# Layer-0 attention scores: one 128-column matmul per head over 64 contraction rows, in place of one 256-column matmul per pair of heads over 128 rows

## The chip, the cores and the metric

The kernel runs on one core of a Trainium2 chip. The metric is the device time of one execution in microseconds (us).

## What is computed

A two-layer Perceiver block, batch 1: 128 queries of width 256 attend to a context of 12544 positions of width 192. Each of the two layers has cross attention, a small self attention and a feed-forward part. The change touches only the cross attention of layer 0 (16 heads of 16 channels, no mask):

```python
x = x + _L0_xattn_ref(_layernorm(x, axis=-1), ctx_768, Wq, bq, Wk, bk, Wv, bv, Wo, bo)

def _L0_xattn_ref(query, key_value, Wq, bq, Wk, bk, Wv, bv, Wo, bo):
    q = (query @ Wq + bq)        # split into 16 heads of 16
    k = (key_value @ Wk + bk)
    v = (key_value @ Wv + bv)
    attn = jnp.einsum('bhqd,bhkd->bhqk', q, k) * scale
    attn = jnp.clip(attn, -CLAMP, CLAMP)
    attn = jax.nn.softmax(attn, axis=-1)
    x = jnp.einsum('bhqk,bhkd->bqhd', attn, v)
    return x @ Wo + bo
```

## The kernel before

The program is written by hand, one instruction stream for each engine, with named semaphores (S["..."]) between them.

**Layer 0 in chunks.** The context is worked through in 14 chunks (NCH) of 896 positions (CH), each chunk in 7 tiles (TPC) of 128 positions. While the scores of chunk c are computed, chunk c+1 is prepared: keys are projected (`project0`, L1319) and values (`values0`, L1326), and an upper estimate of every head's maximum is taken by 32 small matmuls (`unit_scores`, L1336, each over the 32 rows of one pair of heads, 448 columns) whose results VectorE reduces (`unit_max`, L899). The maxima of the chunk go through a matmul (`minus_max_row`, L1345) and a ScalarE copy (`max_row`, L625) into rows of the score operand `qs`, so that the matmul of the scores subtracts them.

**Scores.** Operands are split in a rounded high part and a rest, both kept in the type fp32r. In `ks` and `qs` the products high*high, high*low and low*high are stacked along the contraction: rows 0 to 31, 32 to 63 and 64 to 95 hold the 2 x 16 channels of a pair of heads in three versions, rows 96 to 127 hold ones against the negated maxima. So `scores0` (L1413 to L1421) needs a single matmul per pair of heads: 128 rows, 128 positions (the weights, from `ks`), and 256 columns (the queries of both heads; the queries of the other head are zero in a head's columns). A tile has 8 such matmuls in two halves (z), each half filling two PSUM banks; ScalarE takes the exponential of the two banks in one instruction (`exponentials`, L666).

**Weighing.** `weigh0` (L1430) multiplies the exponentials with the values in plain fp32, which the chip executes as two instructions per matmul: 16 matmuls of 17 weight columns a tile, four of them side by side in the column groups of the array.

**Order.** The table LIST (L76 to L78) sets the order of TensorE's work: S is the scores of the next tile, W the weighing of this one, m one maximum matmul, K, V, F, R, L the other preparing steps. Three PSUM banks (5 to 7) are used in turn by all of K, V, m, F, R and L. In the five middle steps the order is

```python
LIST += [["S", "m", "m", "m", "W", "m", "m"]] * 5
```

in the first step S stands between two K (after K1, before K2), and in the last step it stands behind L and before the next chunk's K0. In that last place the two halves of S each wait (`e0_top`) for ScalarE's copies of the maxima.

**Moving keys to their rows.** A DMA can put data in any partition, so SyncE's queue fills `ks`: `stack_keys` (L313 to L325) issues 12 DMAs a chunk of 32 partitions each (L323), 8 when the high parts of the keys are ready (`e0_khi`) and 4 when the low parts are (`e0_klo`). Behind them on the queue are the loads of a later chunk (`load_sum0`) and the way of the maxima to all partitions (`spread_max`), which only a rarely used clipping path reads. `qs` is filled once by 12 DMAs (L309). GpSimd sets the rows of ones in both halves of `ks` by two memsets (L473, L490).

Of the kernel before, what the change touches and what calls it, by code (L numbers as in the profile page):

```python
# [150 lines left out]
def perceiver(nc, a, out):  # L151
    with ExitStack() as ctx:
# [15 lines left out]
        qs = sb("qs", [P, HQ], F32R)  # L168
# [111 lines left out]
        def _(sp):  # L280
# [26 lines left out]
            for slot, part in ((0, qp[:, :, :, :]), (1, qp_lo), (2, qp[:, :, :, :])):  # L307
                for g in range(4):
                    sp.dma_start(qs_v[32 * slot:32 * slot + 32, :, g, :].bitcast(F32),  # L309
                                 part[32 * g:32 * g + 32].rearrange("p t e q -> p t (e q)").bitcast(F32)  # L310
                                 ).then_inc(S["qs_rows"], 16)

            def stack_keys(c, b):  # L313
# [3 lines left out]
                sp.wait_ge(S["e0_score"], HALVES * (c + 1))  # L317
                for slot, part in ((0, 0), (1, 0), (2, 1)):
                    if slot == 2:
                        carry_wait()  # L320
                        sp.wait_ge(S["e0_klo"], 4 * c + 4)
                    for g in range(4):
                        sp.dma_start(ks_v[32 * slot:32 * slot + 32, b, g::4, :].bitcast(F32),  # L323
                                     khl[32 * g:32 * g + 32, part, :, :].bitcast(F32)
                                     ).then_inc(S[f"e0_keys{b}"], 16)  # L325

            def spread_max(c):
# [4 lines left out]
                sp.dma_start(rows_d, qs[96:97, :].bitcast(F32)).then_inc(S["e0_row_out"], 16)  # L332
# [93 lines left out]
        def _(pool):  # L426
# [50 lines left out]
            pool.wait_ge(S["qs_rows"], 192)  # L477
# [12 lines left out]
            nc.gpsimd.memset(ks[96:P, GROUPS * CH:].bitcast(F32), 1.0).then_inc(S["ks_ones"], 1)  # L490
            pool.wait_ge(S["ks_ones"], 2)
# [85 lines left out]
        def _(act):  # L577
# [81 lines left out]
            def exponentials(c, b, t):  # L659

                for u in (2 * t, 2 * t + 1):
                    g = HALVES * c + u
                    act.wait_ge(S["e0_ok"], g + 1)
                    act.wait_ge(S["e0_score"], g + 29)
# [6 lines left out]
            def chunk0(c, b, i2, nxt=True, split=True, sums=False):  # L671

                for t in range(TPC):
                    for kind, i, n in STEPS[t]:
# [9 lines left out]
                        elif kind == "K":  # L684
                            if i == 0:
                                act.wait_ge(S[f"e0_keys{b}"], 192 * (i2 + 1))
# [6 lines left out]
                        elif kind == "R":  # L693
                            if i % 2 == 0:
                                act.wait_ge(S["e0_score"], HALVES * (c + 1) + 27 + i // 2)
# [1038 lines left out]
```

## Time and profile before

| | |
|---|---|
| median of 3 runs | 980.12 us (979.84 to 983.88) |
| the profiled execution: its own time | 981.7 us |
| its span, first to last instruction | 979.9 us |
| TensorE busy (matmul) | 832.2 us, 85% |
| VectorE / ScalarE / GpSimd busy | 646.0 / 426.7 / 217.2 us |
| mean granted TensorE clock | 0.915 of full speed |

Layer 0's chunks fill the span from about 60 to 531 us; the rest is layer 1 and the short stages between. A duration in the profile is that of one instruction from its start to its end; matmuls overlap, so that their rate is read from when a row of n like instructions starts and how long it lasts, and not from the mean duration.

### The profile page before, as it was taken

What the parts mean: (1) busy time and instruction counts of PE and PEld (TensorE: products, weight loads), DVE (VectorE), ACT (ScalarE), POOL (GpSimd) and SP (SyncE); (2) the same over time, 40 slices, a digit from 0 to 9 for tenths busy, and PEclk for the clock granted to TensorE, in tenths of its full rate; (3) what the DMA queues carried; (4) which work ended last, traced back from release to release, by engine and by line L of the source; (5) the groups of instructions that cost most, each with busy time, mean ns of one, the idle gap of its engine ahead of it and who ended that gap; (6) DMA issues with size and microseconds to landing.
All of it is one profiled execution on the core that took longest, in us unless ns stands there. A gap on an engine that the chain in (4) does not pass through costs nothing. (4 is left out here: it accounts for less than half of the span.)

```text
span 979.9 us, 21240 instructions
## 1 busy us (share of the span) xinstructions
PE 832.2 (85%) x7299; PEld 640.1 (65%) x7299; DVE 646.0 (66%) x1116; ACT 426.7 (44%) x575; POOL 217.2 (22%) x234
## 2 busy tenths in 40 slices
PE   3889999999999999999996166995999999996605
PEld 2567777777777777777775055653788888885304
DVE  5767766856766676676664123895577877785782
ACT  2246676576666667666666022100233323331011
POOL 4162102202211220220104902140132223220000
PEclk9779999999999999999999568997899999998755
DMA  5845654573565557386333003200000000000000
GB/s 169 204 135 126 157 148 127 117 181 104 135 156 138 133 115 177 104 229 156 92 88 113 39 0 124 76 13 0 13 12 18 18 13 17 18 13 0 1 0 6
DMA packets 44152, 85.35 MB, mean 87 GB/s; under 512 B 11648, under 2 KB 26945, under 8 KB 42177
## 3 DMA queue, kind: packets, MB, share of 16 engines
q1 hardware_dynamic: 44110, 84.87, 33.6%
q8 instruction: 18, 0.29, 0.1%
q14 instruction: 24, 0.19, 0.1%
HBM read 45.27 MB, written 0.25 MB: 46 GB/s over the span
## 5 line engine op out<-in xcount | busy, mean ns | idle before, releaser
L899 DVE TENSOR_REDUCE cu<-ps 128x1 f32<-128x448 f32 x448 | 250.4, 618 | 53.2 <-PE ps L1336 51.3
L666 ACT ACTIVATE pr<-ps 128x1024 f32<-128x1024 f32 x196 | 190.1, 1023 | 64.9 <-PE ps L1418 64.1
L432 POOL TENSOR_TENSOR pause<-pause 128x1 f32<-128x1 f32 x41 | 13.0, 317 | 584.7 <-DVE mr L911 376.9
L1418 PE MATMUL ps<-qs,ks 128*128 128x256 f32 x784 | 122.9, 296 | 5.8 <-ACT qs L625 3.1
L1336 PE MATMUL ps<-khl,qp 32*128 32x448 f32 x448 | 123.4, 480 | 3.0 <-DVE khl L889 0.9
L1418 PEld LDWEIGHTS ps<-qs,ks 128*128 128x128 f32 x784 | 102.0, 190 | 24.4 <-issue 20.0
L1430 PE MATMUL ps<-pr,v 128*17 128x128 f32 x3136 | 104.7, 274 | 0.6 <-DVE ps L976 0.5
L1585 PE MATMUL ps<-ks,ct 128*128 128x512 f32 x352 | 99.5, 405 | 2.7 <-ACT ks L769 2.3
L1430 PEld LDWEIGHTS ps<-pr,v 128*17 128x17 f32 x3136 | 77.2, 97 | 22.5 <-issue 19.2
L1336 PEld LDWEIGHTS ps<-khl,qp 32*128 32x128 f32 x448 | 57.5, 186 | 48.8 <-DVE cu L899 14.3
L1179 DVE TENSOR_SCALAR ps<-ps 128x1024 f32<-128x1024 f32 x44 | 54.1, 1229 | 52.8 <-PE ps L1586 52.8
L889 DVE SCALAR_TENSOR_TENSOR khl<-ps,bk,khl 128x448 fp32r<-128x448 f32 x56 | 37.2, 682 | 73.8 <-ACT khl L613 73.7
L780 ACT ACTIVATE pr<-ps 128x1024 f32<-128x1024 f32 x44 | 45.3, 1029 | 84.6 <-DVE ps L1179 84.6
L1585 PEld LDWEIGHTS ps<-ks,ct 128*128 128x128 f32 x352 | 65.7, 192 | 20.6 <-issue 6.2
L1326 PE MATMUL ps<-wv,ct 128*128 128x256 f32 x490 | 73.4, 299 | 4.4 <-DVE cu L899 3.6
L1326 PEld LDWEIGHTS ps<-wv,ct 128*128 128x128 f32 x490 | 65.7, 196 | 15.4 <-DVE cu L899 7.9
L1319 PE MATMUL ps<-ct,wk 128*128 128x448 f32 x280 | 69.2, 388 | 1.7 <-DVE khl L889 1.7
L619 ACT COPY v<-ps 128x256 f32<-128x256 f32 x98 | 36.6, 373 | 60.9 <-PE ps L1326 59.8
L1162 DVE TENSOR_TENSOR pr<-pr,wraw 128x1024 f32<-128x1024 f32 x45 | 55.1, 1224 | 4.0 <-issue 4.0
L1319 PEld LDWEIGHTS ps<-ct,wk 128*128 128x128 f32 x280 | 52.9, 200 | 6.3 <-DVE khl L889 2.3
L1166 DVE TENSOR_TENSOR nm<-nm,pr 128x1024 f32<-128x1024 f32 x45 | 55.4, 1232 | 1.5
L1146 DVE CUSTOM_DVE_ANT_0 pr<-ps,khl 128x1024 f32<-128x1024 f32 x48 | 55.5, 1220 | 0.0
(262 smaller groups left out, 1103.9 us busy)
## 6 DMA issues: line engine op xcount, KB each, us to landing
ks<-khl SPq DMA_DIRECT2D x168, 224.0 KB, 4.9
nm<-maxima SPq DMA_DIRECT2D x14, 1024.0 KB, 4.7
raw<-in_ctxT SPq DMA_DIRECT2D x14, 448.0 KB, 3.8
raw<-in_ctxT SPq DMA_DIRECT2D x28, 224.0 KB, 4.4
ffw<-in_mask_q SPq DMA_DIRECT2D x1, 1568.0 KB, 10.1
raw<-in_ctxT SPq DMA_DIRECT2D x12, 128.0 KB, 2.2
raw<-in_ctxT SPq DMA_DIRECT2D x22, 64.0 KB, 1.8
raw<-in_ctxT SPq DMA_DIRECT2D x44, 32.0 KB, 2.1
```

Source lines behind the costliest of these rows:

```text
L666: nc.scalar.activation(pr[:, (HALVES * b + u) % 4, :], bank(2 * (u % 2), 2), ACT.Exp).then_inc(S["e0_exp"], 1)
L899: V.tensor_reduce(cu2[:, h, half:half + 1], ps[:, use_bank(n), 0:NB], AX_X, ALU.max).then_inc(S["e0_red"], 1)
L1146: nc.vector.tensor_tensor_reduce(out=junk[:, h % 2], in0=ps[:, 2 * (h % 4):2 * (h % 4) + 2, :], in1=negm[:, b, :].bitcast(F32).rearrange(" ...
L1162: V.tensor_tensor(sl, sl, mk[:, u // 2, :].unsqueeze(1).to_broadcast([P, 8, T]), ALU.mult).then_inc(S["e1_masked"], 1)
L1166: V.tensor_tensor(acc, acc, pr[:, u, :], ALU.add).then_inc(S["e1_sum"], 1)
L1179: V.tensor_scalar(bank(2 * (u % 2), 2), bank(2 * (u % 2), 2), 80.0, None, ALU.min).then_inc(S["e1_ok"], 1)
L1319: last = mm(dst, wk0[:, w, t * P:(t + 1) * P], ct[:, b, xx, half * NB:(half + 1) * NB], start=(j == 0), stop=(j == 4))
L1326: last = mm(ps[:, use_bank(n), 0:C], ct[:, b, xx, t * P:(t + 1) * P], wv0[:, w, :], start=(j == 0), stop=(j == 4))
L1336: mm(ps[:, use_bank(n), 0:NB], qp[part, t, e, :], khl[part, 0, t, half * NB:(half + 1) * NB], start=True, stop=True).then_inc(S["e0_head"], 1)
L1418: last = mm(ps[:, 2 * z + k // 2, (k % 2) * 256:(k % 2) * 256 + 256], ks_v[:, b, gg, t * P:(t + 1) * P], qs[:, gg * 256:gg * 256 + 256], s ...
L1430: last = mm(ps[32 * j:32 * j + 17, 4, (h // 4) * T:(h // 4 + 1) * T], v17_v[:, b, t, h, :], pr[:, (HALVES * b + u) % 4, k * T:(k + 1) * T] ...
L1585: mm(ps[:, 2 * z + j, :], cu[:, t, xx, :], asp[:, w, cols], start=(i == 0), stop=False)
```

## The change

The two heads of a pair no longer share a matmul. Rows 0 to 63 of `ks` and `qs` now belong to the first head of a pair, rows 64 to 127 to the second. Inside each half, 16 rows hold high*high, the next 16 high*low, then 16 rows of ones against the negated maximum, then 16 low*high. `scores0` issues a matmul for each head: 64 rows, 128 weight columns, 128 columns of queries; the first head of a pair writes to the half's first bank, the second to its second bank. 16 matmuls a tile stand where 8 stood, and each half now counts `e0_score` up by 2.

`qs` is half as wide. `stack_keys` issues 24 DMAs of 16 partitions instead of 12 of 32, `qs` is filled by 24 instead of 12, and each memset of ones becomes two of 16 rows. The heads' order inside the maxima and in `pr` changes with this; the instructions that use it keep their sizes.

```diff
-        qs = sb("qs", [P, HQ], F32R)
+        qs = sb("qs", [P, HQ // 2], F32R)
...
-            for slot, part in ((0, qp[:, :, :, :]), (1, qp_lo), (2, qp[:, :, :, :])):
+            for row, part in ((0, qp[:, :, :, :]), (16, qp_lo), (48, qp[:, :, :, :])):
                 for g in range(4):
-                    sp.dma_start(qs_v[32 * slot:32 * slot + 32, :, g, :].bitcast(F32),
-                                 part[32 * g:32 * g + 32].rearrange("p t e q -> p t (e q)").bitcast(F32)
-                                 ).then_inc(S["qs_rows"], 16)
+                    for e in range(2):
+                        at, of = 64 * e + row, 32 * g + D0 * e
+                        sp.dma_start(qs_v[at:at + D0, :, g, :].bitcast(F32), part[of:of + D0, :, e, :].bitcast(F32)
+                                     ).then_inc(S["qs_rows"], 16)
...
-                sp.wait_ge(S["e0_score"], HALVES * (c + 1))
-                for slot, part in ((0, 0), (1, 0), (2, 1)):
-                    if slot == 2:
+                sp.wait_ge(S["e0_score"], 2 * HALVES * (c + 1))
+                for row, part in ((0, 0), (16, 0), (48, 1)):
+                    if part == 1:
                         carry_wait()
                         sp.wait_ge(S["e0_klo"], 4 * c + 4)
                     for g in range(4):
-                        sp.dma_start(ks_v[32 * slot:32 * slot + 32, b, g::4, :].bitcast(F32),
-                                     khl[32 * g:32 * g + 32, part, :, :].bitcast(F32)
-                                     ).then_inc(S[f"e0_keys{b}"], 16)
+                        for e in range(2):
+                            at, of = 64 * e + row, 32 * g + D0 * e
+                            sp.dma_start(ks_v[at:at + D0, b, g::4, :].bitcast(F32),
+                                         khl[of:of + D0, part, :, :].bitcast(F32)
+                                         ).then_inc(S[f"e0_keys{b}"], 16)
...
-            nc.gpsimd.memset(ks[96:P, 0:GROUPS * CH].bitcast(F32), 1.0).then_inc(S["ks_ones"], 1)
-            pool.wait_ge(S["ks_ones"], 1)
+            for at in (32, 96):
+                nc.gpsimd.memset(ks[at:at + D0, 0:GROUPS * CH].bitcast(F32), 1.0).then_inc(S["ks_ones"], 1)
+            pool.wait_ge(S["ks_ones"], 2)
...
-                nc.scalar.copy(qs[96:P, 512 * i:512 * i + 512], ps[96:P, bank_of("R", i), :]).then_inc(S["e0_top"], 1)
+                row, z = slice(32 + 64 * (i % 2), 48 + 64 * (i % 2)), i // 2
+                nc.scalar.copy(qs[row, 512 * z:512 * z + 512], ps[row, bank_of("R", i), :]).then_inc(S["e0_top"], 1)
...
                 for k in range(4):
                     gg = 4 * z + k
-                    last = mm(ps[:, 2 * z + k // 2, (k % 2) * 256:(k % 2) * 256 + 256],
-                              ks_v[:, b, gg, t * P:(t + 1) * P], qs[:, gg * 256:gg * 256 + 256],
-                              start=True, stop=True)
-                last.then_inc(S["e0_score"], 1)
+                    for e in range(2):
+                        part = slice(64 * e, 64 * e + 64)
+                        last = mm(ps[:, 2 * z + e, k * T:(k + 1) * T],
+                                  ks_v[part, b, gg, t * P:(t + 1) * P], qs[part, gg * T:(gg + 1) * T],
+                                  start=True, stop=True)
+                        if k == 3:
+                            last.then_inc(S["e0_score"], 1)
...
-                    j = h % 4
+                    j, at = h % 4, (4 * (k % 2) + k // 2) * T
                     last = mm(ps[32 * j:32 * j + 17, 4, (h // 4) * T:(h // 4 + 1) * T],
-                              v17_v[:, b, t, h, :], pr[:, (HALVES * b + u) % 4, k * T:(k + 1) * T],
+                              v17_v[:, b, t, h, :], pr[:, (HALVES * b + u) % 4, at:at + T],
                               start=False, stop=True, skip_group_check=True)
```

Waits on `e0_score`, `e0_keys0` and `e0_keys1`, `qs_rows` and `ks_ones` have their counts doubled.

TensorE's stream, first step of a chunk, before: between the two K1 and K2 projections (L1319, full array) stand the two halves of S (L1418); L1352 is F and L1430 the weighing.

```order
L1319 MATMUL ps<-ct,wk 128x448 x5
L1308 ISA
L1352 MATMUL ps<-con,wraw 128x128 x4
L1308 REGISTER_ALU
L1319 MATMUL ps<-ct,wk 128x448 x5
L1415 ISA
L1418 MATMUL ps<-qs,ks 128x256 x4
L1415 REGISTER_ALU
L1418 MATMUL ps<-qs,ks 128x256 x4
L1300 ISA
L1319 MATMUL ps<-ct,wk 128x448 x10
```

The same place after the change (the projections are L1329 now, the scores L1430):

```order
L1329 MATMUL ps<-ct,wk 128x448 x5
L1318 ISA
L1362 MATMUL ps<-con,wraw 128x128 x4
L1318 REGISTER_ALU
L1329 MATMUL ps<-ct,wk 128x448 x5
L1425 ISA
L1430 MATMUL ps<-qs,ks 128x128 x8
L1425 REGISTER_ALU
L1430 MATMUL ps<-qs,ks 128x128 x8
L1310 ISA
L1329 MATMUL ps<-ct,wk 128x448 x10
```

Nothing has changed its place; two runs of 4 matmuls have become two of 8, with half the columns.

SyncE's queue in one pass of the chunk loop, before (L323 is `stack_keys`, L282 the loads, L332 the maxima):

```order
L323 DMA ks<-khl 32x2x896 x12
L298 REGISTER_ALU
L282 ISA
L282 DMA raw<-in_ctxT 128x896
L282 ISA
L282 DMA raw<-in_ctxT 64x896 x2
L331 REGISTER_ALU
L332 DMA maxima<-qs 1x2048
```

and after:

```order
L326 DMA ks<-khl 16x2x896 x24
L298 REGISTER_ALU
L282 ISA
L282 DMA raw<-in_ctxT 128x896
L282 ISA
L282 DMA raw<-in_ctxT 64x896 x2
L334 REGISTER_ALU
L335 DMA maxima<-qs 2x2x512
```

The order is the same here too; 24 transfers of half the size are issued where there were 12.

## Rows read from the trace of the kernel before

**Rows 1.** Stretches: us; busy us (instructions) of PE, PEld, DVE, ACT, POOL; clock; DMA; GB/s.

```profile
74.00:545.00 471.00, 449.17 (x5160) 348.31 (x5160) 314.50 (x644) 310.79 (x436) 92.49 (x56) 0.99 0.54 137
...
321.81:325.07 3.26, 3.26 (x50) 2.40 (x46) 2.75 (x6) 1.95 (x3) 0.00 (x0) 1.00 0.98 195
```

**Rows 2.** Timeline of PE, one middle step: start us, length us, line, form, count.

```profile
321.81 0.73 PE L1336 MATMUL ps<-khl,qp 32*128 32x448 f32 x2
322.47 1.22 PE L1418 MATMUL ps<-qs,ks 128*128 128x256 f32 x8
323.62 0.52 PE L1336 MATMUL ps<-khl,qp 32*128 32x448 f32 x3
324.07 1.07 PE L1430 MATMUL ps<-pr,v 128*17 128x128 f32 x32
325.07 0.73 PE L1336 MATMUL ps<-khl,qp 32*128 32x448 f32 x2
325.73 1.22 PE L1418 MATMUL ps<-qs,ks 128*128 128x256 f32 x8
```

**Rows 3.** Timeline of DVE, the same step; in brackets idle before it and its releaser.

```profile
320.87 2.75 DVE L899 TENSOR_REDUCE cu<-ps 128x1 f32<-128x448 f32 x5 [0.50 <-PE ps L1336]
324.12 1.16 DVE L899 TENSOR_REDUCE cu<-ps 128x1 f32<-128x448 f32 x2 [0.51 <-PE ps L1336]
```

**Rows 4.** Timeline of PE, a chunk's end and the next one's first step.

```profile
303.37 0.73 PE L1418 MATMUL ps<-qs,ks 128*128 128x256 f32 x4 [0.24 <-ACT qs L625]
303.94 1.18 PE L1319 MATMUL ps<-ct,wk 128*128 128x448 f32 x5
304.95 1.05 PE L1352 MATMUL ps<-con,wraw 128*128 128x128 f32 x8
...
306.86 1.12 PE L1418 MATMUL ps<-qs,ks 128*128 128x256 f32 x8
307.82 2.21 PE L1319 MATMUL ps<-ct,wk 128*128 128x448 f32 x10
```

**Rows 5.** Groups by form: busy us, mean ns of one, idle before them and its releasers.

```profile
L1418 PE MATMUL ps<-qs,ks 128*128 128x256 f32 x784 | 122.9, 296 | 5.8 <-ACT qs L625 3.1 <-ACT pr L666 2.7
L1418 PEld LDWEIGHTS ps<-qs,ks 128*128 128x128 f32 x784 | 102.0, 190 | 24.4 <-issue 20.0 <-ACT pr L666 3.8
L1430 PEld LDWEIGHTS ps<-pr,v 128*17 128x17 f32 x3136 | 77.2, 97 | 22.5 <-issue 19.2 <-ACT pr L666 1.9 <-DVE ps L976 0.7
```

**Rows 6.** Line L1336: durations min/median/max in ns, first and last start.

```profile
L1336 PEld LDWEIGHTS ps<-khl,qp x448: 181/181/284, 29.6 to 504.7; 32*128 32x128 f32 x150
L1336 PE MATMUL ps<-khl,qp x448: 460/467/738, 29.6 to 504.7; 32*128 32x448 f32 x150
```

**Rows 7.** Timeline of PE, two maximum matmuls before a score block.

```profile
328.79 0.47 PE L1336 MATMUL ps<-khl,qp 32*128 32x448 f32 x2
329.19 1.21 PE L1418 MATMUL ps<-qs,ks 128*128 128x256 f32 x8
```

**Rows 8.** Line L1533, a 64-row fp32 matmul of layer 1: the same columns as rows 6.

```profile
L1533 PE MATMUL ps<-v,pr x64: 272/272/373, 601.1 to 608.6; 64*128 64x128 f32 x64
```

**Rows 9.** Chain of waits, in order of time: start us, us, what.

```profile
601.11 3.85 PE ps L1533 x32
```

**Rows 10.** Timeline of the SP queue around two sets of key copies.

```profile
276.39 10.02 SPq L323 DMA_DIRECT2D ks<-khl  x12
297.91 1.74 SPq L282 DMA_DIRECT2D raw<-in_ctxT  x3
...
310.86 10.28 SPq L323 DMA_DIRECT2D ks<-khl  x12
```

**Rows 11.** DMA issues: line, count, KB each, median us from issue to landing.

```profile
ks<-khl SPq DMA_DIRECT2D x168, 224.0 KB, 4.9
```

**Rows 12.** Timeline of POOL at the start; in brackets idle before.

```profile
18.76 6.23 POOL L473 MEMSET ks<- 32x7168 f32 x1
44.99 0.19 POOL L432 TENSOR_TENSOR pause<-pause 128x1 f32<-128x1 f32 x1 [20.00 <-DVE mr L911]
```

More of the change, by code:

```diff
@@ L331, in spread_max @@
                 sp.wait_ge(S["e0_nm"], 16 * c)
-                sp.dma_start(rows_d, qs[96:97, :].bitcast(F32)).then_inc(S["e0_row_out"], 16)
+                sp.dma_start(rows_d.rearrange("o (z e n) -> (o e) z n", z=2, e=2),
+                             qs[32:97:64, :].rearrange("p (z n) -> p z n", z=2).bitcast(F32)
+                             ).then_inc(S["e0_row_out"], 16)
                 sp.wait_ge(S["e0_row_out"], 16 * c + 16)
@@ L489, in _ @@
                 pool.wait_ge(S["mask_halved"], n)
-            nc.gpsimd.memset(ks[96:P, GROUPS * CH:].bitcast(F32), 1.0).then_inc(S["ks_ones"], 1)
-            pool.wait_ge(S["ks_ones"], 2)
+            for at in (32, 96):
+                nc.gpsimd.memset(ks[at:at + D0, GROUPS * CH:].bitcast(F32), 1.0).then_inc(S["ks_ones"], 1)
+            pool.wait_ge(S["ks_ones"], 4)
             with pool.Fori(2, NCH, 2) as c:
@@ L663, in exponentials @@
                     act.wait_ge(S["e0_ok"], g + 1)
-                    act.wait_ge(S["e0_score"], g + 29)
+                    act.wait_ge(S["e0_score"], 2 * (g + 29))
                     act.wait_ge(S["e0_pv"], g + 11)
@@ L685, in chunk0 @@
                             if i == 0:
[L686 removed]
+                                act.wait_ge(S[f"e0_keys{b}"], 384 * (i2 + 1))
                                 act.wait_ge(S["e0_head"], UNITS * (c + 1))
@@ L694, in chunk0 @@
                             if i % 2 == 0:
-                                act.wait_ge(S["e0_score"], HALVES * (c + 1) + 27 + i // 2)
+                                act.wait_ge(S["e0_score"], 2 * (HALVES * (c + 1) + 27 + i // 2))
                                 act.wait_ge(S["e0_row_out"], 16 * (c + 1))
@@ L927, in after_maxima @@
                 dve.wait_ge(S["e0_spread"], c)
-                V.tensor_tensor(fall[:, :], mr[:, 1 - b, :].bitcast(F32), mr[:, b, :].bitcast(F32), ALU.subtract
+                old, new = (mr[:, j, :].rearrange("p (z e k) -> p z e k", z=2, e=2).bitcast(F32) for j in (1 - b, b))
+                V.tensor_tensor(fall[:, :].rearrange("p (z k e) -> p z e k", z=2, e=2), old, new, ALU.subtract
                                 ).then_inc(S["e0_fall"], 1)
@@ L983, in clip_half @@
                     dve.wait_ge(S["e0_nm"], 16 * c + 16)
-                dve.wait_ge(S["e0_score"], k + 29)
+                dve.wait_ge(S["e0_score"], 2 * (k + 29))
                 V.scalar_tensor_tensor(s, nm[:, 1024 * z:1024 * z + 1024], CLAMP, s, ALU.add, ALU.min
@@ L1263, in _ @@
             mm = nc.tensor.matmul
-            pe.sem_inc(S["e0_score"], 28)
+            pe.sem_inc(S["e0_score"], 2 * 28)
             pe.sem_inc(S["m1_head"], 32)
@@ L1359, in large_sum, with tile @@
                 mm(ps[:, use_bank(n), 0:1], ones, large[:, :], start=True, stop=True).then_inc(S["e0_flag"], 1)
-            def tile(c, b, count, t, ones=2):
+            def tile(c, b, count, t, ones=4):
                 for z in range(2):
@@ L1365, in tile @@
                         pe.wait_ge(S["ks_ones"], ones)
-                        pe.wait_ge(S[f"e0_keys{b}"], 192 * count)
+                        pe.wait_ge(S[f"e0_keys{b}"], 384 * count)
                         pe.wait_ge(S["e0_top"], 4 * c + 2 * z + 2)
@@ L1442, in _ @@
                 step0(-1, 1, None, t, first=True)
-            pe.wait_ge(S["qs_rows"], 192)
-            tile(0, 0, 1, 0, ones=1)
+            pe.wait_ge(S["qs_rows"], 384)
+            tile(0, 0, 1, 0, ones=2)
             with pe.Fori(0, (NCH - 2) // 2) as i2:
@@ L1720 @@
             where[:, None] == where[None, :], where[:, None] <= where[None, :], np.ones((P, P)),
-            np.abs(where[:, None] - where[None, :]), np.repeat(-1.0 * (where[None, :] == 96), P, axis=0),
+            np.abs(where[:, None] - where[None, :]), np.repeat(-1.0 * (where[None, :] % 64 == 32), P, axis=0),
             where[:, None] // D0 == np.arange(8)[None, :],
```

5 lines of the change are left out of this document (3 added, 2 removed).

## The prediction

> **What bounds the kernel now.** I read the stretches first: in the 471 us of layer 0's chunks TensorE has a matmul under way for 449 us at a granted clock of 0.99, so at its upper level of 2.4 GHz, VectorE for 315 and ScalarE for 311 [rows 1]. TensorE is the engine to follow. Then the timeline of one middle step: score block, three maximum matmuls, weighing, two maximum matmuls, and again from 322.47 to 325.73, a period of 3.26 us [rows 2]. VectorE works 2.75 us of it and stands still for 0.51 us, just behind the score block, waiting for the first maximum matmul [rows 3]. So the loop runs through the score block: what it loses or gains comes through one for one, until VectorE's 0.5 us a step are used up. At a chunk's border and in its first step TensorE runs without a gap from 303.37 on [rows 4]. There are 14 chunks of about 34.5 us (276.39 to 310.86, the key copies of two chunks [rows 10]), 7 score blocks each, 98 in all (784 matmuls of 256 columns, 8 a block) [rows 5].
>
> **Price of a score matmul now.** 8 of them last 1.12 us [rows 4], the last one 0.282 us of it, so one follows the other every 0.12 us. 256 columns at 2.4 GHz, one a cycle, are 0.107 us; 0.013 us come on top. The weight load beside it lasts 190 ns for 128 weight columns and 97 ns for the 17 of the weighing [rows 5], that is 0.84 ns a column, so a full load occupies the array's weight path for some 0.107 us and the rest of its 190 ns is latency. A load of only 32 rows lasts 181 ns [rows 6]: the rows hardly matter, the columns do. Now, load and stream take the same time and hide each other.
>
> **Price after.** A 128-column matmul streams for 0.053 us but still needs a load of 128 columns. Within one row half it can follow its predecessor no faster than the load allows. The nearest rows of that pace are F's, 8 full loads in 1.05 us with 0.275 us for the last, 0.111 us each [rows 4], and the 64-row fp32 matmuls of L1533, which load 128 columns each: 32 of them in 3.85 us with 0.272 us for the last, 0.115 us each [rows 8, 9]. I take 0.111 us; the ends are 0.12 us (the fp32r pace of now) and 0.067 us (0.053 + 0.013, if a 64-row load were no bound).
> The two row halves should run side by side. Two maximum matmuls of different row groups last 0.47 us together, first start to last end [rows 7], and a single one lasts 0.467 us [rows 6]: loads and streams of both overlap wholly. So a block is 8 pairs at 0.111 us, not 16 matmuls in a row.
>
> **Price of changing the shape.** Between maximum matmuls a block costs more than its matmuls: from its start to the next maximum matmul 1.15 us (322.47 to 323.62) [rows 2], against 0.96 us (306.86 to 307.82) between two full-array projections [rows 4]. Likewise the pair before the block starts 0.40 us ahead of it [rows 7], though its 448 columns stream in 0.187 us. Both fit one reading: on a change of the rows in use TensorE empties (about 0.1 us) and then loads the first weights in the open (0.107 us), some 0.21 us a change. The block is 0.108 load + 7 x 0.12 + 0.107 stream + 0.1 emptying = 1.155 us. The Trainium skill, "TensorEngine Tiling (Array Packing)", Key Properties, says that a change of the tiling mode drains the engine while a change of the tile alone doesn't; by that rule the 64-row blocks still pay on both sides of the 32-row ones, and newly pay beside the 128-row projections. The trace agrees as far as it goes (32 to 128 rows and back, 0.2 us each); 64 rows beside others it doesn't show.
>
> **The sum, per chunk.**
> - Five blocks between maximum matmuls: 0.108 + 7 x 0.111 + 0.053 + 0.1 = 1.04 us for 1.155, so -0.117 each, **-0.59 us**.
> - The block between K1 and K2, today without a shape change: from the end of K1's stream to the start of K2's it takes 0.012 + 7 x 0.12 + 0.12 = 0.97 us; after, (0.1 + 0.108) + 7 x 0.111 + 0.053 + (0.1 + 0.108) = 1.25 us: **+0.28 us**.
> - The block at the chunk's border: its first half gets a shape change too, but the second half waits for ScalarE's copies of the maxima anyway (0.24 us of idle) [rows 4], which hides it. From that release: 0.108 + 3 x 0.12 + 0.12 = 0.59 us now, 0.108 + 3 x 0.111 + 0.053 + 0.21 = 0.70 us after: **+0.11 us**.
>
> Together -0.20 us a chunk. In the last chunk no maxima are taken and ScalarE sets half of the pace; I count it as nothing. 13 x -0.20 = -2.6 us. With 0.12 us a pair it is +2.7 us; with new shape changes of double cost (three a chunk, 13 x 3 x 0.21) +5.6, with free ones -10.8.
>
> **What moves beside it.** Copies of the keys: 12 issues take 10.02 us of SyncE's queue now, 0.84 each, with the DMA engines at a share near 1 then (0.98) [rows 1, 10]; so the bytes set the pace, and they stay the same. 24 issues need 10 us by bytes, 20 us if an issue has a fixed price. The next thing on the queue, the load of the context, starts 11.5 us after the last issue [rows 10], so even 20 us delay nothing there, and keys issued from 276.39 land 4.9 us after their issue [rows 11], at 301.3, before their first reader shortly ahead of 303.37 [rows 4]. I count 0. At the start 12 more DMAs for `qs` and 12 for the keys fall ahead of the first scores, at worst some 2 us once; the likelier value is 0. The memset of ones takes 6.23 us for 7168 elements a row, whatever the rows, so it doubles, and GpSimd has 20.00 us of idle behind the first [rows 12]: 0. The copies of maxima keep their length (512 elements a row), ScalarE's exponential its two banks, VectorE's small operations their size: 0. The second count of `e0_score` in a half is an update without a wait: 0.
>
> The profiled execution took 981.7 us, 1.6 above the median; 981.7 - 2.6 = 979.1 there, and against the median 980.1 - 2.6 = **977.5 us**. Of this kernel a measurement can tell about 0.5%, 4.9 us, from no change: the forecast is "the same". Its own range, from the ends above, is 970 to 988.
>
> **Rivals.**
> 1. *Slower: the halves don't overlap in a long run, or a 128-column fp32r matmul isn't one pass.* The trace shows pairs side by side, never a run of eight pairs in which one half's load must be pulled ahead of the other half's waiting matmul. If it isn't, a pair costs two loads, 0.222 us: 1.72 us a block of pairs for 0.83, +0.89 on some 91 unhidden blocks (13 x 7) = +81, so 1059 us. If narrow fp32r matmuls cost as much as fp32 ones, two instructions of 0.111 us each [rows 4] in either half, it is +86, so 1063 us. It decides as soon as a pair exceeds about 0.12 us. Against the second: all fp32r matmuls here have 256 columns or more, at one column a cycle, so nothing shows narrow ones slow or fast. For the first: loads are pulled ahead between column groups (32 weighing instructions in 1.07 us, four to a load and stream of 0.11) [rows 2]. Chance 0.12.
> 2. *Slower: the key copies come late.* 16 partitions might move at less than the rate of 32. Between first issue and first reader lie about 26 us, less 4.9 to land: 21.1 us for 24 issues, 0.88 each, against 0.84 now. At 0.95 us it costs 1.7 us a chunk, 13 times 22 us: 1000 us. Chance 0.04.
> 3. *Faster: only the columns count.* With 0.067 us a pair a block is 0.36 us shorter than forecast (8 x 0.044), x 91 = -32 us: 945 us. The 181 ns load of 32 rows [rows 6] speaks against it. Chance 0.04. The Trainium skill, same page, Theoretical Speedup, has up to twice the speed for a contraction of at most 64 rows; that would be this case or better, and the trace's load durations don't agree with it for blocks of 128 columns.
> 4. *Faster: 32-row and 64-row matmuls follow each other without emptying.* Two changes at each of five blocks, 13 x 10 x 0.2 = -26: 951 us. Both directions now cost 0.2 us, so chance 0.04.
> 5. *Slower by a little:* the new shape changes cost more than 0.21 us, or the start loses its 2 us and more; 985 to 1000 us. Chance 0.06.
>
> **Numbers.** Forecast 0.70, of which 0.14 lies below 975.2 and 0.05 above 985.0. Faster by over 0.5%: 0.14 + 0.04 + 0.04 = 0.22. Slower: 0.05 + 0.12 + 0.04 + 0.06 = 0.27. Within: 0.51. The range 970 to 1000 holds the forecast, rival 5 and the late keys (0.70 + 0.06 + 0.04 = 0.80).
>
> **What would show it.** In the changed profile 1568 score matmuls of 64 rows; in a middle step a block from its start to the next maximum matmul in 1.04 us (1.09 at the slow end; 1.9 under rival 1; 0.7 under rival 3); gaps of 0.2 us beside the block in the first step, where there is none now; a chunk's period of 34.3 us for 34.5; 24 key issues in 10 to 20 us, with the wait of the scores still on the copies of the maxima and not on a DMA. If the score instructions count 3136, narrow fp32r isn't one pass. If the period of a middle step falls by more than 0.12 us, the price of the load or of the shape change is wrong.

## The result and the profile after

| | before | changed |
|---|---|---|
| runs, median (range) | 980.25 us (979.84 to 983.88, 4 runs) | 1013.8 us (1009.56 to 1017.98, 4 runs) |
| profiled execution, its span | 981.7, 979.9 us | 1017.98, 1016.2 us |
| mean granted clock | 0.915 | 0.900 |

The ratio is 1.0334, 95% interval 1.0271 to 1.0396: slower by 33.6 us, where 977.5 us and "the same" were forecast. The forecast's range ended at 1000.

The page of the changed kernel first: section 2 (tenths of busy time and of the granted clock), section 3 (queues), section 5 (groups).

```profile
PE   1889989989989989989999625899599999997604
...
PEclk9859989989989989989999557999799999998755
...
q8 instruction: 65, 1.06, 0.5%
...
L1430 PE MATMUL ps<-qs,ks 64*128 64x128 f32 x1568 | 115.4, 284 | 7.6 <-ACT qs L633 5.5
L1430 PEld LDWEIGHTS ps<-qs,ks 64*128 64x128 f32 x1568 | 99.2, 191 | 29.6 <-issue 25.7
...
L1329 PE MATMUL ps<-ct,wk 128*128 128x448 f32 x280 | 80.9, 436 | 17.8 <-issue 16.1
```

And the same rows of the kernel before:

```profile
PE   3889999999999999999996166995999999996605
...
PEclk9779999999999999999999568997899999998755
...
q8 instruction: 18, 0.29, 0.1%
...
L1319 PE MATMUL ps<-ct,wk 128*128 128x448 f32 x280 | 69.2, 388 | 1.7 <-DVE khl L889 1.7
```

The score matmuls (L1430, L1418 before) are what was forecast: 1568, one instruction each, and less busy time in sum (115.4 us for 122.9 [rows 5]). The news is elsewhere. In the chunk loop (slices 3 to 21) TensorE's busy time and its clock have a dent every third slice, about every 75 us. The key projections, which the change does not touch, last 11.7 us more and stand behind 16.1 us of idle with releaser "issue". The queue that fetches instructions moved 65 packets (16 KB each) instead of 18.

TensorE's timeline of the changed kernel at one dent, and then the stretches around it (columns as in rows 1):

```profile
287.90 0.66 PE L1430 MATMUL ps<-qs,ks 64*128 64x128 f32 x8 [0.41 <-ACT qs L633]
292.05 2.23 PE L1329 MATMUL ps<-ct,wk 128*128 128x448 f32 x5 [3.49 <-issue]
294.08 1.91 PE L1362 MATMUL ps<-con,wraw 128*128 128x128 f32 x8
295.64 2.01 PE L1329 MATMUL ps<-ct,wk 128*128 128x448 f32 x5
297.58 1.11 PE L1430 MATMUL ps<-qs,ks 64*128 64x128 f32 x16
```

```profile
288.56:292.05 3.49, 0.00 (x1) 0.01 (x1) 0.00 (x0) 1.72 (x2) 0.00 (x0) 0.77 0.42 115
292.05:298.62 6.57, 6.57 (x35) 5.83 (x35) 0.95 (x2) 2.08 (x4) 0.00 (x0) 0.60 0.26 105
298.62:303.11 4.49, 4.17 (x47) 2.95 (x46) 3.08 (x6) 2.87 (x4) 0.00 (x0) 1.00 0.00 0
```

The last score block of a pass is done at 288.56. Then TensorE has nothing for 3.49 us, no engine's data being late, and when it resumes, its first matmuls run at 1.2 GHz: the factors (L1362) take 1.91 us where they took 1.05 [rows 4]. Mean clock of that stretch 0.60, then 1.00 again. This happens where the loop of TensorE's program branches back (L1459), each time. One whole pass of two chunks, from key projection to key projection, first before, then changed:

```profile
269.37:338.44 69.07, 67.74 (x764) 52.73 (x763) 47.32 (x96) 46.37 (x67) 12.40 (x8) 1.00 0.55 137
```

```profile
292.05:366.96 74.91, 70.05 (x875) 54.62 (x875) 47.65 (x96) 47.12 (x66) 12.38 (x8) 0.96 0.59 127
```

+5.84 us a pass. Counting TensorE's records in the trace between two branches gives what the pass issues: before 762 matmuls, 762 weight loads and 176 register, semaphore and branch instructions, 1700 recorded instructions; after 874, 874 and 176, 1924. The packets of the instruction queue fall accordingly: before, none lies between 125 and 477 us, in which passes 2 to 6 run; after, 9 lie in each of these passes. There are five branches back. Of the 36.3 us between the spans, 5.6 stand ahead of the first chunk's key projection (67.24 us for 61.60), and most of the rest is five times 5.8.

The 5.6 us at the start are another thing. VectorE, then GpSimd, then TensorE of the changed kernel:

```profile
18.39 6.09 DVE L884 CAST qp<-v 128x512 fp32r<-128x512 f32 x1
...
18.14 12.36 POOL L479 MEMSET ks<- 16x7168 f32 x2
...
25.52 0.59 PE L1452 MATMUL ps<-zero 128*128 128x512 bf16 x1 [12.38 <-DVEq L886]
```

And before:

```profile
16.81 2.18 DVE L876 CAST qp<-v 128x512 fp32r<-128x512 f32 x1
...
20.02 0.59 PE L1439 MATMUL ps<-zero 128*128 128x512 bf16 x1 [6.58 <-DVEq L878]
```

The memset started 0.25 us ahead of VectorE's cast of the queries, and the cast ended 0.2 us after the first of the two memsets (24.48 against 18.14 + 6.18). Before, the cast had started before the memset (18.76 [rows 12]) and took 2.18 us. Both kernels can meet this: in e12 below, a form of the kernel before, the memset starts at 17.01 and the cast, 0.26 us behind it, takes 6.09 us too. The Trainium skill, "SBUF — State Buffer", SBUF: two separate sides, describes a port pair that VectorE and GpSimd take exclusively for a whole instruction. These rows agree with it.

VectorE is held up in the kernel before as well. The first line is its next wide step there, the others are the same start in e7 below, which is the kernel before once more:

```profile
19.86 5.17 DVE L882 TENSOR_SCALAR mr<-mx 128x16 fp32r<-128x16 f32 x1
```

```profile
14.36 0.43 DVE L876 CAST qp<-v 128x512 fp32r<-128x512 f32 x1
...
17.41 1.81 DVE L882 TENSOR_SCALAR mr<-mx 128x16 fp32r<-128x16 f32 x1
```

With no GpSimd instruction running ahead of it the cast lasts 0.43 us; its 2.18 us in the kernel before end at 18.99, 0.3 us behind such an instruction (L457, 16.57 to 18.70). L882, which touches 16 elements a row, ends at 25.03 with the memset (18.76 + 6.23). In the changed kernel VectorE waits through both memsets: the same step (L890) ends at 30.53, the second memset at 30.50. So VectorE gets to the first keys (L889, L897 after) at 22.25 us in e7's profile, 25.39 in before's and 30.89 in the changed kernel's. e7's profiled run took 976.18 us where that of before took 981.7, with the same program, and the 5.5 us between them are all there at the second chunk's key projection (91.23 and 96.71 us).

### The profile page after: what moved, and what is told of

It is laid out like the page before. It is cut to its first block and busy times, and to the rows that moved or that the text cites. A ratio compares the mean times of both kernels' runs of the same rounds, so it can differ in the third digit from the quotient of the medians.

```text
span 1016.2 us, 22993 instructions
## 1 busy us (share of the span) xinstructions
PE 844.8 (83%) x8081; PEld 651.7 (64%) x8083; DVE 653.5 (64%) x1116; ACT 431.5 (42%) x575; POOL 229.0 (23%) x236
## 3 DMA queue, kind: packets, MB, share of 16 engines
q8 instruction: 65, 1.06, 0.5%
## 5 line engine op out<-in xcount | busy, mean ns | idle before, releaser
L437 POOL TENSOR_TENSOR pause<-pause 128x1 f32<-128x1 f32 x41 | 12.4, 303 | 607.8 <-DVE mr L919 402.8
L1430 PE MATMUL ps<-qs,ks 64*128 64x128 f32 x1568 | 115.4, 284 | 7.6 <-ACT qs L633 5.5
L1430 PEld LDWEIGHTS ps<-qs,ks 64*128 64x128 f32 x1568 | 99.2, 191 | 29.6 <-issue 25.7
L897 DVE SCALAR_TENSOR_TENSOR khl<-ps,bk,khl 128x448 fp32r<-128x448 f32 x56 | 38.1, 682 | 109.3 <-ACT khl L620 108.6
L1443 PE MATMUL ps<-pr,v 128*17 128x128 f32 x3136 | 106.8, 278 | 0.6 <-DVE ps L986 0.6
L1329 PE MATMUL ps<-ct,wk 128*128 128x448 f32 x280 | 80.9, 436 | 17.8 <-issue 16.1
L1336 PE MATMUL ps<-wv,ct 128*128 128x256 f32 x490 | 73.6, 299 | 4.4 <-DVE cu L907 3.6
L1329 PEld LDWEIGHTS ps<-ct,wk 128*128 128x128 f32 x280 | 59.8, 227 | 25.1 <-issue 16.8
L1336 PEld LDWEIGHTS ps<-wv,ct 128*128 128x128 f32 x490 | 66.0, 196 | 15.3 <-DVE cu L907 7.9
L620 ACT ACTIVATE khl<-ps,bk 128x448 fp32r<-128x448 f32 x56 | 35.6, 636 | 50.2 <-PE ps L1329 48.8
```

What stands on the lines that cost most here:

```text
L1329: last = mm(dst, wk0[:, w, t * P:(t + 1) * P], ct[:, b, xx, half * NB:(half + 1) * NB], start=(j == 0), stop=(j == 4))
L1336: last = mm(ps[:, use_bank(n), 0:C], ct[:, b, xx, t * P:(t + 1) * P], wv0[:, w, :], start=(j == 0), stop=(j == 4))
L1430: last = mm(ps[:, 2 * z + e, k * T:(k + 1) * T], ks_v[part, b, gg, t * P:(t + 1) * P], qs[part, gg * T:(gg + 1) * T], start=True, stop=True)
L1443: last = mm(ps[32 * j:32 * j + 17, 4, (h // 4) * T:(h // 4 + 1) * T], v17_v[:, b, t, h, :], pr[:, (HALVES * b + u) % 4, at:at + T], start= ...
```

## The experiments

**Is it the place of the loop, or its length?** The first theory (A) was that a loop of 1924 instructions no longer fits into what TensorE keeps of its program, or fits only at some positions in memory. e1, e2 and e3 shift the loop by 64, 128 and 192 instructions:

```
             pe.wait_ge(S["w0_lo"], 1)
+            for _ in range(64):
+                pe.sem_inc(S["shift"], 1)
```

> Edit: the changed kernel with 64 semaphore increments ahead of TensorE's chunk loop, in a place where it waits anyway; the loop's instructions are the same, only where they lie in memory is moved by 64 instructions. In the changed kernel's trace one pass of the loop is 1924 recorded TensorE instructions and 9 transfers of 16 KB on the instruction queue fall into its 75 us, where the kernel before has 1700 and none; each pass begins with some 3.5 us in which TensorE waits for nothing that the profile shows. Theory A (the code of the loop doesn't stay with the engine, 9 blocks of 16 KB where only fewer are held): the time depends on where the body lies against the block borders, so this shift either changes nothing (still 9 blocks, 1009 to 1018 us) or takes all transfers out of the loop and gives about 978 us (six passes of some 5.9 us less). Theory B (the loss comes from the 24 key copies or another wait that the change brings): no shift changes anything, 1009 to 1018 us with all three shifts. The Trainium skill, page on NRT and kernel launch, has 128 KB of instruction memory for TensorE in blocks of 16 KB, 8 blocks; by that a body of 1924 instructions of 64 bytes (7.5 blocks) fits in about half of all positions.

> As the shift by 64, by 128 instructions. Theory A: of the positions unmoved, 64, 128 and 192 one or two of four must lie well (a body of 7.5 blocks touches 8 blocks or 9); such a position has no instruction transfers inside the loop and some 978 us, the others 1009 to 1018 us. Theory B: 1009 to 1018 us.

> As the shift by 64, by 192 instructions. Theory A: about 978 us or unchanged; at least one of the three shifts must be fast. Up to some 5 us can come on top here, since so many increments may last longer than the wait they stand in. Theory B: 1009 to 1018 us.

| | us | ratio (interval) | instruction fetches |
|---|---|---|---|
| e1 | 1015.52 | 1.0379 (1.0339 to 1.0419) | 65 |
| e2 | 1020.86 | 1.0421 (1.0385 to 1.0458) | 70 |
| e3 | 1027.36 | 1.0489 (1.0454 to 1.0524) | 66 |

No position is fast. What e2 and e3 have on top is paid ahead of the first matmul, where the increments stand (16.0 and 26.1 us of idle there, for 12.4 in the changed kernel; I had allowed 5 us for it in e3, and it took 13.6). The idle at the branch stays, here in e1's and e3's list of waits (us in total, times, longest):

```profile
PE ps L1329 <- issue: 15.9, 5, 3.4
```

**Is it the branch?** e4 writes TensorE's loop out:

```
-            with pe.Fori(0, (NCH - 2) // 2) as i2:
+            for i2 in range((NCH - 2) // 2):
```

> Edit: in the changed kernel TensorE's six passes of the chunk loop are written out one after the other, with no branch back. Theory A in its narrow form (a branch back to code that is gone costs the wait, code fetched in sequence doesn't): every block is still fetched, about 45 more transfers than before the change, but the 3.5 us at each pass's start vanish: about 978 us. Theory A in its wide form (each block fetched costs TensorE time wherever it comes): stays slow, 990 to 1015 us. Theory B: 1009 to 1018 us.

Measured 985.41 us (983.83 to 989.19), ratio 1.0057 (1.0036 to 1.0078), 7 us above the 978 of the expectation. 28 of the 33.6 us are gone with the branch. The code still comes in by 55 fetches, and no idle of L1329 is put down to "issue" any more: code that runs straight on is fetched in time. A pass:

```profile
272.00:341.29 69.29, 67.53 (x876) 52.50 (x874) 47.63 (x96) 46.91 (x67) 12.40 (x8) 1.00 0.69 138
```

e5 is its control, the kernel before with the same edit:

> The kernel before, with TensorE's chunk loop written out by Python's range as in e4, and nothing else. Theory A (what costs the change its time is the branch back to code that is no longer there, and the loop of the kernel before, 1700 recorded TensorE instructions a pass, is still there at each branch): before has no such stall to lose, so 980.1, ratio 1.000 within 0.003; writing out is then free, and what e4 had over before (1.0057) belongs to the change itself. Rival B (a loop that is written out is faster by itself, since it loses the branches and their register sums): below 977, and then e4 overstates what the change can be worth without its stall.

980.35 us, ratio 1.0001 (0.9977 to 1.0026), with 48 fetches: writing out is free and gains nothing that the times show (in the trace a chunk takes 34.48 us for 34.52).

**Is it length alone?** e6 and e7 were to lengthen the loop of the kernel before by matmuls that are jumped over:

> The kernel before, with its own scores, copies and memsets, and 160 further matmuls in TensorE's loop body between the two chunks, behind a condition that is never true (they are jumped over; the output is unchanged). They add some 320 instructions to the span of the loop's code, which then is about as long as after's or longer. Theory A (length of the loop's code alone): the profile shows 9 or more instruction fetches a pass of two chunks, an idle of TensorE of 3 to 4 us with releaser issue at the first key projection of each pass, the granted clock at half behind it, and 1005 to 1020 us in all, ratio 1.025 to 1.04. Rival C (the fetches of after come of something in its matmuls, their tile positions or banks, not of the length of the code): the jump costs under 0.3 us a pass and the time is 980 to 983.

> The same as e6 with 16 matmuls behind the never-true condition instead of 160: the jump is there, the code grows by some 32 instructions only, to about 1735 a pass. Theory A: no fetches in the loop, 980 to 983 us (ratio 1.000 to 1.003). If the conditional jump were what costs, this run is as slow as e6.

1.0003 (0.9983 to 1.0022) and 0.9993 (0.9970 to 1.0017), with 18 fetches each. They say nothing on length: the condition was known false when the program was built, and the block was left out of it. Both are the kernel before again. e9 makes it true in the last pass:

```
+                    if b == 0:
+                        with pe.If(i2 > 4):
+                            for _ in range(240):
+                                pe.sem_inc(S["shift"], 1)
```

> In e6 and e7 the condition was known to be false when the kernel was built and nothing of the added block was left in TensorE's program: they were the kernel before once more. Here the condition (pass number above 4) is true in the last of the six passes alone, and the block holds 240 increments of a semaphore that nobody waits for, between the two chunks of TensorE's loop: the code of a pass grows from 1700 to about 1940 instructions, as long as after's, and in five of six passes they are jumped over. Theory A (length of the loop's code alone): 8 or more instruction fetches a pass, an idle of TensorE of 3 us or more with releaser issue once or more a pass, the pass 72 to 76 us instead of 69.1, and 1000 to 1018 us in all. Rival C (the matmuls of the change bring the fetches): passes one to five keep 69.1 to 69.4 us, no fetches between 143 and 420 us, and the time is 980 to 990, with the block's own execution in the last pass.

> e9 with 112 increments in the jumped block instead of 240: the code of a pass is about 1815 instructions, between before's 1700 (stays) and after's 1924 (does not). It brackets the length that stays. If 1815 stays: passes one to five 69.1 to 69.4 us with no fetches, and what is over 980 in all is the block's own execution in the last pass, up to 17 us by e9's 36 us for 240, so 985 to 998. If it does not: passes of 73 to 75 us as in e9 and 1010 to 1030 in all. I expect the second, at 55 percent, since shifts of the loop by up to 192 instructions never made 1924 fit.

> The control of e9 and e12: the same jump at the same place of the kernel before, over 16 increments instead of 240 or 112; the code of a pass is about 1720 instructions. Theory A (length): passes one to five 69.1 to 69.5 us, 18 or 19 instruction fetches in all, 981 to 985 us with up to 2.4 us for the block's own execution. Rival J (a jump taken forward costs the fetches, whatever it jumps over): passes of 74 to 75 us and over 1005.

One pass in which the block is jumped over, from key projection to key projection, in e9 (code of 1941 instructions), e12 (1813) and e13 (1717):

```profile
276.63:351.95 75.32, 70.49 (x762) 54.97 (x763) 47.31 (x96) 46.65 (x66) 12.40 (x8) 0.95 0.52 130
```

```profile
287.24:362.85 75.61, 70.71 (x763) 55.21 (x763) 47.29 (x96) 46.74 (x66) 12.39 (x8) 0.95 0.52 129
```

```profile
265.81:334.84 69.03, 67.70 (x764) 52.70 (x763) 47.31 (x96) 46.42 (x67) 12.42 (x8) 1.00 0.56 137
```

and the start of the same e9 pass:

```profile
276.63 2.23 PE L1319 MATMUL ps<-ct,wk 128*128 128x448 f32 x5 [2.95 <-issue]
```

The kernel before, with its own matmuls and nothing more executed in these passes, gets the idle, the half clock and 6.3 and 6.5 us in the pass shown, once its loop body is long (64 fetches in all, 9 in every pass). The idle stands at the branch back; at the forward jump, ahead of the key projection at 313.70 in e9, there is none. With the same jump over 16 instructions it has none of this (18 fetches). In all, e9 took 1049.45 us (1.0707, 1.0670 to 1.0744), e12 1030.54 (1.0501, 1.0473 to 1.0529) and e13 986.62 (1.0043, 1.0019 to 1.0067); e9 and e12 also pay for executing the block in the last pass, 36.5 and 16.9 us as the longest idle of L1319. I had put the block's own cost in e9 too low. e13's median lies above the 981 to 985 expected, though its passes are as expected: its ten runs fall into 980.2 to 982.3 and 986.6 to 988.5, and the profiled one (982.33) is of the first kind. e12 went the way I had given 55 percent: 1813 do not stay, 1717 do. Length is the cause, and the 1700 of the kernel before stood at most 113 instructions under the edge. One thing is not separated: what a jump over 112 instructions does in a loop that would fit. The changed kernel itself has no such jump and shows the same 9 fetches a pass at 1924.

The Trainium skill, "Runtime: NRT & Kernel Launch", Instruction fetch mechanics, has it that a taken branch to code outside a window of two pages forces a fetch before the engine can go on, and that sequential code is fetched ahead. e9 agrees with the forced fetch and e4 with the fetching ahead, but the window is not what the runs show: the 1700 instructions of the kernel before, more than six of the section's pages of 256, branch back without a fetch. The section's size of the whole instruction memory for TensorE is 2048 instructions, and by that 1813 and 1924 would fit; these loops stop fitting between 1717 and 1813, and the runs decide.

**What is left without the stall?** e8 keeps the memsets behind VectorE's cast, on top of e4:

```
+            pool.wait_ge(S["qp"], 1)
             for at in (32, 96):
                 nc.gpsimd.memset(ks[at:at + D0, 0:GROUPS * CH].bitcast(F32), 1.0).then_inc(S["ks_ones"], 1)
```

> The change with TensorE's loop written out (e4), and GpSimd waits for VectorE's queries (the semaphore that SyncE waits for too) before its first two memsets of the ones' rows, so that they cannot stand beside the cast of the queries. Theory D (in the profiled run of the change the cast took 6.09 us since it ran beside the memset, and in a part of the runs the same happens; it starts the first matmul 6 us late): no run of this kernel above 988, fastest and slowest within 4 us of each other, median 984 to 985 like e4's fast runs, or 1 to 2 us more where the memsets now end after the query rows are wanted. If the memset delay is not what splits the change's runs into 1010 and 1018, the spread stays as it was.

984.61 us (982.0 to 988.02), ratio 1.0035 (1.0009 to 1.0061). The memsets start at 19.97 us and the cast takes 2.18, but it took 2.18 in e4's profile too, and the spread (6 us) is no smaller than e4's (5.4). The edit moved the meeting instead of removing it: the first memset now holds VectorE's next step (L891, 6.13 us, until 26.07), and the first keys are reached at 26.43 us, for 25.14 in e4. That the cast behind the memset splits the change's own runs into about 1010 and 1018 us is likely, not shown: the profiled runs with the cast at 6.09 us were the slowest of four in the changed kernel (1017.98) and in e12 (1034.43), the one of e1 with 2.18 the fastest of four (1011.66); e2's, with 6.09, lies in the middle of four that differ by 3 us.

The rest stands in the chunks. Lengths by starts, medians over eleven chunks each, e4 against before: first step up to its first maximum matmul 7.38 us for 7.02; middle steps 3.15 for 3.26 in three, 3.21 for 3.25 in one and 3.46 for 3.46 in one; last step with the border 6.14 for 5.97. A chunk is 34.65 us for 34.52 (34.48 in e5, which is written out too). e4's first chunk has 1.9 us more on top (37.01 for 35.11), most of it since the clock is at half for longer: here before and e4 in the stretch 60 to 70 us.

```profile
60.00:70.00 10.00, 9.95 (x79) 8.74 (x79) 3.51 (x7) 7.58 (x11) 6.19 (x2) 0.85 0.26 106
```

```profile
60.00:70.00 10.00, 10.00 (x59) 9.03 (x60) 2.05 (x4) 6.75 (x10) 9.89 (x3) 0.66 0.60 164
```

Why it rises later there no run shows, and it is not the change's alone: the mean clock of that stretch is 0.68 in e5, whose first chunk takes 35.86 us, and 0.77 in e11, whose first chunk takes 35.60.

e10 and e11 move the first step's score block from between the key blocks behind them, in the kernel before and in e8:

```
-LIST = [["K0", "F", "K1", "S", "K2", "K3", "W", "m", ...
+LIST = [["K0", "F", "K1", "K2", "K3", "S", "W", "m", ...
```

> The kernel before with one entry of the order list moved: the score block of the first step behind the fourth key block instead of between the second and the third. Control for e11. In the trace of before the transitions there cost little (score block 0.960 us, shorter than the 1.15 between maxima), so theory B (key blocks and score blocks in the 64-row form disturb each other at their borders, in the 128-row form they hardly do) gives no gain here: 979 to 983, ratio 0.999 to 1.003; it may lose a little, since ScalarE's exponentials of that block start some 2 us later.

> e8 with the same entry of the order list moved as in e10. Theory B (in e4 a chunk has 0.36 us more in the first step than before: each key block that borders on the 64-row score block takes 0.09 us longer, and the score block 0.077): with the score block behind the fourth key block one such border goes, so 0.1 to 0.25 us a chunk less, 981.5 to 983.5 in all, ratio to e8 0.997 to 0.999, and the profile shows the second key block back at 1.10 us. Rival F (the first step waits for VectorE or ScalarE, and what TensorE loses there is only their pace): as e8, 984 to 985, or slower since the exponentials start later, like e10 against before.

982.79 us, 1.0018 (0.9996 to 1.0040), and 984.55, 1.0040 (1.0022 to 1.0059), e8 having 984.61. The gain of 0.1 to 0.25 us a chunk did not come. In the first step of e11

```profile
236.17 1.28 PE L1330 MATMUL ps<-ct,wk 128*128 128x448 f32 x5
237.29 1.05 PE L1363 MATMUL ps<-con,wraw 128*128 128x128 f32 x8
238.10 3.44 PE L1330 MATMUL ps<-ct,wk 128*128 128x448 f32 x15
241.47 1.11 PE L1431 MATMUL ps<-qs,ks 64*128 64x128 f32 x16
242.51 1.07 PE L1444 MATMUL ps<-pr,v 128*17 128x128 f32 x32
243.51 0.47 PE L1347 MATMUL ps<-khl,qp 32*128 32x448 f32 x3
```

the stretch from 236.17 to 243.51 is 7.34 us, 0.04 under e4's 7.38; in e10 it is 7.26 (201.83 to 209.09), 0.24 over before's 7.02. So the 64-row form costs 0.36 us between the key blocks and 0.08 behind them; the borders of e11's theory B are real. But the place behind them costs 0.24 us by itself (e10), nearly all that it saves, and rival F's result is what the times show.

e14 takes up the border of chunks. There TensorE's idle for ScalarE's copies of the maxima rose from 0.24 [rows 4] to 0.41 us. From the third chunk on, e14 puts the first copy of each pair on the partitions of the second, into columns that nothing reads, so that half of the heads keep an older maximum: it is a probe of the timing, not the same computation.

```
                 row, z = slice(32 + 64 * (i % 2), 48 + 64 * (i % 2)), i // 2
+                if not (isinstance(c, int) and c < 2) and i % 2 == 0:
+                    row, z = slice(96, 112), z + 2
```

> e8 with the first of the two copies of maxima in each pair read from partitions 96 to 111 instead of 32 to 47 (and written to spare columns there, so that one head of each pair keeps the first maximum: the computation is changed in that). Theory G (copies one after the other on different partitions of ScalarE follow each other 0.60 us apart, on the same ones 0.49 us, and TensorE waits for the second at the border): the pair takes 1.06 us again, TensorE's idle before the second half of the border's score block falls from 0.41 to about 0.25 us, and the chunk from 34.65 to 34.53 us, 982.5 to 983.5 in all, ratio to e8 0.998 to 0.999. Rival H (the distance comes of the copies' shape or of the maxima's two banks): 34.65 us a chunk and 984 to 985.

ScalarE's pair of copies and TensorE's second half of the border block, in e8 and then in e14:

```profile
266.69 1.18 ACT L634 CAST qs<-ps 16x512 fp32r<-16x512 f32 x2 [1.99 <-PE ps L1356]
...
270.65 0.66 PE L1431 MATMUL ps<-qs,ks 64*128 64x128 f32 x8 [0.43 <-ACT qs L634]
```

```profile
267.55 1.06 ACT L636 CAST qs<-ps 16x512 fp32r<-16x512 f32 x2 [1.99 <-PE ps L1358]
...
271.38 0.66 PE L1433 MATMUL ps<-qs,ks 64*128 64x128 f32 x8 [0.31 <-ACT qs L636]
```

On the same partitions the pair takes 1.06 us as before, TensorE waits 0.12 us less, and the chunk falls from 34.65 to 34.54 us. Each copy lasts 0.58 us in both; it is the second one's start that moves, from 0.60 to 0.49 us behind the first. Theory G holds by the trace; a pair that stays on partitions 32 to 47 was not run. The times do not resolve it: 985.29 us, 1.0028 (1.0010 to 1.0046), above e8's median where 982.5 to 983.5 was expected.

No version ran that beats the kernel before. With the stall and this 0.12 us gone the changed chunk equals the old one, 34.54 us for 34.52. In e14's profile the key projection of the first chunk starts 0.9 us later than before and that chunk is 1.7 us longer; this is most, not all, of what is left.

## Why the prediction was wrong

- **The step that failed** is not one of the terms of the sum but its list, "What moves beside it". The list counted what each engine executes and what moves on the queues of data, and left out that 112 more matmuls, each with its weight load, lengthen TensorE's loop code from 1700 to 1924 instructions a pass. The hint stood in the profile of before: 18 instruction fetches in all (q8), none of them in the loop's passes 2 to 6, so the code was staying resident and could stop doing so. The price, found with e4: 1013.8 − 985.4 = 28 of the 36 us between forecast and result; by the traces, five branches at 5.6 us (74.91 for 69.29 a pass), 3.1 to 3.5 of it idle and the rest the half clock behind it.
- **No rival** named it. Rival 5 (985 to 1000) had the right side for another reason, and the measured time lies beyond it.
- **Five middle blocks, −0.59 us a chunk.** The block's price was right: 313.22 to 314.26 is 1.04 us, as forecast. The gain was right in three of the five (−0.11), a third of that in one, and nothing in another; −0.38 in all. In the lines below, the steps from 310.02 and 313.22 take 3.20 and 3.15 us; the one from 316.37 is that without a gain.

```profile
310.02 1.17 PE L1430 MATMUL ps<-qs,ks 64*128 64x128 f32 x16
...
313.22 1.11 PE L1430 MATMUL ps<-qs,ks 64*128 64x128 f32 x16
314.26 0.63 PE L1346 MATMUL ps<-khl,qp 32*128 32x448 f32 x3
...
316.37 1.11 PE L1430 MATMUL ps<-qs,ks 64*128 64x128 f32 x16
317.41 1.10 PE L1346 MATMUL ps<-khl,qp 32*128 32x448 f32 x3
```

  In that one VectorE has no 0.5 us to spare. It first combines the maxima of half the heads (L915 to L919) and then works without a gap, in e4

```profile
293.86 3.29 DVE L907 TENSOR_REDUCE cu<-ps 128x1 f32<-128x448 f32 x6
```

  so the three maximum matmuls behind the block stretch by what the block saved (1.00 us before, 1.10 after). The prediction took one middle step's slack for all of them.
- **The block between K1 and K2, +0.28 us:** by the starts of e4, K1 has +0.09, the block +0.08 and K2 with K3 +0.09, together +0.26: the mechanism (a shape change costs) and its size were right. The whole first step has +0.36, since K0, which follows the block at the border, has +0.10 as well.
- **The border, +0.11 us:** +0.16, and with that 0.10 of K0 +0.26. The shape change has the forecast size: from the release to K0 0.59 us for 0.57, and the 0.10. What was missing is the second copy of the maxima, which comes 0.12 us later: "The copies of maxima keep their length" is true of one copy and false of the pair (e14).
- **Sum per chunk −0.20:** +0.13, so +1.7 us over 13 chunks instead of −2.6. With 1.9 us in the first chunk that is about e4's +3.7 us of span (983.6 for 979.9).
- **Copies of the keys, 0:** right. In the chunk shown 24 issues took 17.44 us, inside the forecast 10 to 20, and the next load starts after their end, at 323.03.

```profile
301.78 17.44 SPq L326 DMA_DIRECT2D ks<-khl  x24
323.03 1.73 SPq L282 DMA_DIRECT2D raw<-in_ctxT  x3
```

- **Memsets, 0:** wrong in the profiled execution. GpSimd's idle covers its own time, but not the VectorE operations that wait for the memsets to end (the cast and L890): 5.6 us there. The second memset costs this since the 32 rows of ones now lie in two groups of 16, each as long to fill as the 32 had been.

## What to carry to other kernels

When a change turns one instruction into several inside a hardware loop, count the instructions of the loop body on that engine, and look whether the instruction queue is silent while the loop runs: a body that has been resident and grows past the limit (here between 1717 and 1813 recorded instructions) costs a stall at every branch, and on TensorE the half clock after it. Writing the loop out removed that and cost nothing here. Take slack step by step, not from one typical step, and price idle on GpSimd only after asking which VectorE operation runs beside it.

## What the runs showed of the hardware

- TensorE's loop body of 1717 recorded instructions stayed resident, 1813 did not (there with a jump over 112 of them in it); the 1924 of the change did not at any of four positions.
- An absent loop start costs 3.0 to 3.5 us of idle, and then some 2.4 us through the half clock (37.07 us for the first chunk of the pass, 292.05 to 329.12, against 34.67 in e4); straight-line code of the same length costs nothing (e4, e5: 55 and 48 fetches).
- Executing 240 semaphore increments in a row held TensorE for 36.5 us, 112 for 16.9: 0.15 us each, in loops whose code was fetched anew. 16 of them in e13, with no fetch in that pass, held it for 2.0 us, 0.13 each, so most of this price is the increments' own.
- Two ScalarE copies of 512 elements take 1.18 us when the first is on partitions 32 to 47 and the second on 96 to 111, and 1.06 us when both are on 96 to 111 (e14, where the first copy's columns of `qs` are others too).
- Matmuls in the two row halves overlap in long runs: 16 of them (8 pairs) in 1.11 us, a pair about every 0.11 us, the pace of one 128-column weight load. Two halves did not make it faster than that.
- VectorE operations between SBUF tiles waited for GpSimd instructions to end: the same cast of 128x512 took 0.43 us (e7, e9, e13), 2.18 us up to the end of a GpSimd tensor_tensor instruction, and 6.09 us behind a memset of 6.2 us (changed kernel, e2, e12). A GpSimd memset of 7168 elements a row took 6.23 us over 32 rows and 6.2 over 16.
